# One count product and one copy for both neuron layers, and the middle turns written out

## What is computed

```python
def lif(x):                              # over time
    v = v + (xt - v) / TAU               # TAU = 2
    s = spike(v - VTH)                   # VTH = 1
    return (v * (1.0 - s), s)
x = x + lif(time_mix(layer_norm(x, ln1_s, ln1_b), ...))      # layer 0
x = x + lif(channel_mix(layer_norm(x, ln2_s, ln2_b), ...))   # layer 1
...
x = x + _layernorm(_L0_attn_ref(_layernorm(x), ...))
h = silu(lin(x, w1)) * lin(x, w2)
h = gelu(lin(h, h1)); h = gelu(lin(h, h2)); y = lin(h, w3)
x = x + _layernorm(_L0_ffn_ref(_layernorm(x), ...))
```

## Time and profile before

| what | value |
|---|---|
| runs, us | 679.1, 675.87, 678.21 (median 678.21) |
| profiled execution, span, us | 675.9 |
| instructions in the span | 10747 |
| granted TensorE clock, mean | 0.962 |
| busy, share of span: PE, DVE, ACT, POOL | 87%, 81%, 79%, 64% |
| DVE before the copy of `fired_all` (L1168), waiting for PE's sum | 40.2 us, 31 times |
| eight loop turns, us | 293.14 |
| the two turns after them, written out, us | 73.46 |

### The profile page before, as it was taken

The page is one execution under the profiler, slowest core; times in us unless marked ns, Lnnn a source line. Parts: engine busy times, 40 slices in busy tenths (PEclk is TensorE's granted clock), DMA queues, the critical chain, the costliest instruction groups (busy, mean ns, idle before and its releaser), DMA issues. The chain is left out here.

```text
span 675.9 us, 10747 instructions
## 1 busy us (share of the span) xinstructions
PE 587.6 (87%) x2241; PEld 365.2 (54%) x2241; DVE 549.4 (81%) x1532; ACT 536.8 (79%) x849; POOL 433.9 (64%) x576
## 2 busy tenths in 40 slices
PE   1246489999999999999999999999999999989783
PEld 0022146566655656575656665665657565656562
DVE  2865878989898998989898989899898989775631
ACT  4846377988989897979798898989797979857672
POOL 4323554687778685877768777868587774745352
PEclk9858889999999999999999999999999999999996
DMA  6110010001010100001010101010000101000000
GB/s 222 62 32 2 1 32 16 17 17 32 17 32 16 33 16 13 18 16 31 16 31 16 31 16 31 16 31 15 18 17 0 32 2 31 17 1 16 1 16 16
DMA packets 26538, 16.81 MB, mean 25 GB/s; under 512 B 1152, under 2 KB 25728, under 8 KB 26240
## 3 DMA queue, kind: packets, MB, share of 16 engines
q1 hardware_dynamic: 26496, 16.34, 7.9%
HBM read 12.14 MB, written 4.19 MB: 24 GB/s over the span
## 5 line engine op out<-in xcount | busy, mean ns | idle before, releaser
L780 ACT ACTIVATE hid<-p_f,scale 128x512 f32<-128x512 f32 x128 | 87.9, 687 | 64.9 <-PE p_f L1721 64.4
L1721 PE MATMUL p_f<-a_lo,w_hi 128*128 128x512 f32 x320 | 133.2, 416 | 3.0 <-DVE a_lo L293 1.7
L1721 PE MATMUL p_f<-a_hi,w_hi 128*128 128x512 f32 x320 | 125.9, 393 | 0.0
L1721 PE MATMUL p_f<-b_lo,w_hi 128*128 128x512 f32 x256 | 111.9, 437 | 3.6 <-DVE b_lo L293 2.3
L1721 PE MATMUL p_f<-b_hi,w_hi 128*128 128x512 f32 x256 | 100.5, 393 | 0.0
L427 POOL TENSOR_TENSOR rstd<-var,minus_half 128x4 f32<-128x4 f32 x64 | 84.9, 1326 | 2.5
L774 ACT ACTIVATE a_hi<-hid 128x512 fp32r<-128x512 f32 x128 | 79.1, 628 | 3.2 <-DVE hid L1260 1.5
L443 POOL TENSOR_TENSOR nd<-factors,pq 128x512 f32<-128x512 f32 x32 | 39.2, 1224 | 54.6 <-DVE pq L1127 54.5
L293 DVE TENSOR_TENSOR a_lo<-hid,a_hi 128x512 fp32r<-128x512 f32 x96 | 64.5, 696 | 10.5 <-ACT a_hi L774 10.4
L1721 PEld LDWEIGHTS p_f<-a_lo,w_hi 128*128 128x128 f32 x320 | 60.2, 188 | 23.1 <-issue 8.8
L293 POOL TENSOR_TENSOR b_lo<-hid,b_hi 128x512 fp32r<-128x512 f32 x32 | 46.5, 1467 | 39.1 <-ACT b_hi L774 34.7
(11 more groups left out here) (141 smaller groups left out, 1451.2 us busy)
## 6 DMA issues: line engine op xcount, KB each, us to landing
xa<-in_x SPq DMA_DIRECT2D x16, 256.0 KB, 2.8
xb<-in_x SPq DMA_DIRECT2D x16, 256.0 KB, 3.0
out<-y_out SPq DMA_DIRECT2D x16, 256.0 KB, 3.0
kk<-in_ffn SPq DMA_DIRECT2D x1, 1024.0 KB, 6.0
hid<-in_ffn SPq DMA_DIRECT2D x1, 1024.0 KB, 8.4
mix<-in_mix SPq DMA_DIRECT2D x1, 512.0 KB, 6.2
gate<-in_ffn SPq DMA_DIRECT2D x1, 512.0 KB, 4.0
mix<-in_mix SPq DMA_DIRECT2D x1, 320.0 KB, 3.8
```

Of the source, the lines that this page charges most:

```text
L780: act.activation(hid[:, m], p_f[m % 2][:, :], ACT.Gelu, scale=scale[:, 1 + layer, m:m + 1]).then_inc(s_gelu[layer], 1)
L1721: last = pe.matmul(out_, w[:, b], x[:, k], start=(k == 0 and t == 0), stop=(k == n - 1 and t == len(terms) - 1))
```

## The change

Two things are done.

First, `fired` and `fired_all` are one tile of two columns each, with one semaphore for the sum and one for the copy. `fired_sum` is one product of both columns for each turn, at the place where `fired_sum(1)` stood; it waits for both `fire`. `fired_flags` is one copy of two numbers behind `mix_1(0)`, where `fired_flag(0)` stood. Both `neurons` wait for that copy. POOL clears `fired` once at the start (one more memset, so the count of constants is 12).

Second, the loop is gone: turns 6 to 13 are written out with constants, on every engine. `g.edge` keeps PE's additional waits to the turns outside 6 to 13, where they were before.

```diff
-    def __init__(self, pair, step):
+    def __init__(self, pair, step, edge=True):
...
-        fired = [sb(f"fired{k}", [P, 1], BF16) for k in range(2)]
-        fired_all = [sb(f"fired_all{k}", [P, 1]) for k in range(2)]
+        fired = sb("fired", [P, 2], BF16)
+        fired_all = sb("fired_all", [P, 2])
...
             for i in range(first, last + 1):
-                if i == loop[0]:
-                    with fori(loop[0] // 2, len(loop) // 2 + loop[0] // 2) as pair:
-                        turn(groups(pair, 0), on(6))
-                        turn(groups(pair, 1), on(7))
-                elif i not in loop:
-                    which = first_turn if i < 3 else turn if i < GROUPS else last_turn
-                    which(groups(i // 2, i % 2), on(i))
+                which = first_turn if i < 3 else turn if i < GROUPS else last_turn
+                which(groups(i // 2, i % 2, not 6 <= i < GROUPS - 2), on(i))
...
             def neurons(k, g):
-                pool.wait_ge(s_fired_all[k], g.n + 1)
+                pool.wait_ge(s_fired_all, g.n + 1 + k)
                 pool.wait_ge(s_h_in[k], g.n + 1)
...
-            def fired_flag(k, g):
-
-                dve.wait_ge(s_fired_sum[k], g.n + 1)
-                wait(dve, s_spikes[k], g.n)
-                dve.tensor_copy(fired_all[k][0:1, :], p_m[0][0:1, 2 * k:2 * k + 1]).then_inc(s_fired_all[k], 1)
+            def fired_flags(g):
+
+                dve.wait_ge(s_fired_sum, g.n + 1)
+                wait(dve, s_spikes[0], g.n)
+                wait(dve, s_spikes[1], g.n - 1)
+                dve.tensor_copy(fired_all[0:1, :], p_m[0][0:1, 0:2]).then_inc(s_fired_all, 1)
...
                 if on[3]:
                     fire(1, g[3])
-                    fired_flag(1, g[3])
                 if on[2]:
                     fire(0, g[2])
                 if on[1]:
                     mix_1(g[1], 0)
-                if on[2]:
-                    fired_flag(0, g[2])
+                if on[2] or on[3]:
+                    fired_flags(g[2])
...
+                def fired_sum(g):
+
+                    after(pe, s_h_in[1], g.n - 1)
...
+                    after(pe, s_fired[0], g.n)
+                    after(pe, s_fired[1], g.n - 1)
+                    pe.matmul(p_m[0][:, 0:2], ones16[:, :], fired[:, :], start=True, stop=True).then_inc(s_fired_sum, 1)
...
-                    if on[3]:
-                        fired_sum(1, g[3])
+                    if on[2] or on[3]:
+                        fired_sum(g[2])
                     if on[4]:
                         hidden(1, g[4], 2)
-                    if on[2]:
-                        fired_sum(0, g[2])
                     if on[3]:
                         spikes_turned(1, g[3])
```

More of the change, by code:

```diff
@@ L50, in __init__ @@
         self.turn = pair + step // 2
+        self.edge = edge
 def after(eng, sem, n, per=1, nth=1):
[L55 to L59, removed]
+    if n < 0:
+        return
+    if n >= GROUPS_IN_ALL:
+        n, nth = GROUPS_IN_ALL - 1, per
     eng.wait_ge(sem, per * n + nth)
 def wait(eng, sem, count):
-    if not isinstance(count, int) or count > 0:
+    if count > 0:
         eng.wait_ge(sem, count)
@@ L248, in build @@
         s_spikes = [sem(f"s_spikes{k}") for k in range(2)]
-        s_fired_sum = [sem(f"s_fired_sum{k}") for k in range(2)]
-        s_fired_all = [sem(f"s_fired_all{k}") for k in range(2)]
+        s_fired_sum = sem("s_fired_sum")
+        s_fired_all = sem("s_fired_all")
         s_spk_tok = [sem(f"s_spk_tok{k}") for k in range(2)]
@@ L309, in build, with schedule, groups @@
         block = ctx.enter_context(nc.Block())
-        def schedule(fori, first_turn, turn, last_turn, first=-2, last=GROUPS + 3):
+        def schedule(first_turn, turn, last_turn, first=-2, last=GROUPS + 3):
             def on(i):
                 return {k: 0 <= i - k < GROUPS for k in range(-2, 5)}
-            def groups(pair, step):
-                return {k: Group(pair, step - k) for k in range(-2, 5)}
-            loop = range(6, GROUPS - 2)
+            def groups(pair, step, edge):
+                return {k: Group(pair, step - k, edge) for k in range(-2, 5)}
             for i in range(first, last + 1):
-                if i == loop[0]:
-                    with fori(loop[0] // 2, len(loop) // 2 + loop[0] // 2) as pair:
-                        turn(groups(pair, 0), on(6))
-                        turn(groups(pair, 1), on(7))
-                elif i not in loop:
-                    which = first_turn if i < 3 else turn if i < GROUPS else last_turn
-                    which(groups(i // 2, i % 2), on(i))
+                which = first_turn if i < 3 else turn if i < GROUPS else last_turn
+                which(groups(i // 2, i % 2, not 6 <= i < GROUPS - 2), on(i))
         @block.sync
@@ L361, in turn @@
             def turn(g, on):
-                if not isinstance(g[0].n, int) or 1 <= g[0].n < GROUPS - 2:
+                if 1 <= g[0].n < GROUPS - 2:
                     load_a(g[-2])
-                if on[0] and (not isinstance(g[0].n, int) or g[0].n > 0):
+                if on[0] and g[0].n > 0:
                     load_b(g[0])
@@ L634, in last_turn @@
                     shift_2(g[1])
-            schedule(pool.Fori, first_turn, turn, last_turn)
+            schedule(first_turn, turn, last_turn)
         @block.scalar
@@ L741, in relu @@
                 wait(act, s_fv, g.n)
-                if isinstance(g.n, int) and g.n == 0:
+                if g.n == 0:
                     act.wait_ge(s_rest[0], 1)
@@ L1004, in last_turn @@
                     inverse(g[1])
-            schedule(act.Fori, first_turn, turn, last_turn)
+            schedule(first_turn, turn, last_turn)
         @block.vector
@@ L2063, in last_turn @@
                         turn_5(g[4])
-                schedule(pe.Fori, first_turn, turn, last_turn, **turns)
+                schedule(first_turn, turn, last_turn, **turns)
             program(False, last=2)
```

145 lines of the change are left out of this document (62 added, 83 removed).

## The result

The changed kernel takes 693.97 us (median of four runs, 692.57 to 694.36) against 678.54 us for the kernel before on the same chip (675.87 to 679.1): the ratio is 1.0228, with an interval of 1.0204 to 1.0252. It is 15.4 us slower. The forecast was 681.2 us, with a range from 674.4 to 686.8, so the direction was right and the size far off.

What follows compares the result with a forecast made beforehand. The prediction took a ring of waits, not one full engine, to bound the kernel; -0.5 + 0.7 + 1.0 + 1.8 = +3.0 us on the median 678.21 gave 681.2 us, range 674.4 to 686.8.

Steps and rivals of the forecast that it cites:

- The waits as slack: DVE's waits before the copies (`fired_all`, 40.2 us, 2.62 per turn) are no gain: DVE would wait before `add_2` instead.
- the list of expected signs: Signs if right: 40.2 us shrink, waiting returns before `add_2`, middle turns 36.7 to 37.0 us, turn 3 longer by 1 to 1.5.
- PE's order sets this place: `add_2` and `add_1` on DVE wait for PE's turned tiles, dated by PE's place in its order, which the change leaves untouched.
- The second sum, -0.5: On PE, dropping the second sum saves 0.04 us in each of 12 full turns: -0.5 us.
- The loop, +0.7: Turns 6 to 13 written out take 36.73 us each instead of 36.64: +0.7 us, with ends -2.3 and +2.3.
- Rival 2: All turns take the short length, every `rstd(4)` at 1.39 us; faster, 674.9 us; chance 0.20.
- rival 4: The loop's jump back stalls engines, so writing it out gives back 2.3 us: 678.2 us; chance 0.04.
- The start-up, +1.0: In turn 3 the first transpose comes 1.5 us late, with nothing to fill in: +1.0 us, ends 0 and +1.5.
- Where the one copy falls, cost 0: The copy behind `mix_1(0)` ends at 512.80, allowing the transpose at 513.62, which PE reaches at 513.95: cost 0.
- 0.3 us of cover: Margin before PE's first transpose; if it goes, every further 0.1 us is 0.1 us of the turn.
- rival 1: POOL's `residual_5` takes the ports before `mix_1(0)`, transpose 0.67 us late: +9.2 in all, 687.4 us; chance 0.12.
- the freed POOL's 1.8 us: POOL's `low(2,0)` runs ahead of DVE's `low(2,1)`, making it 0.10 to 0.40 late: 0.15 × 12 = +1.8 us.

Runs made afterwards that it cites:

- The last experiment: Changed kernel with copy ahead of the mixing, transposes earlier, stats_3 ahead of low(2,1), residual_5 behind rstd(2): 684.94 us, ratio 1.0084 against the kernel before.

## Why the prediction was right or wrong

- **The waits as slack: right.** The 40.2 us before the copies were not to be had; DVE's waiting came back before `add_2`, with the transpose named, as the list of expected signs said. That PE's order sets this place holds: with the transposes earlier, `add_2` came 0.8 us sooner. The last experiment adds that the arm through hidden(1,3) and ACT's high part is only some 0.6 us shorter, and grows when the transposes move.
- **The second sum, -0.5: nothing.** The written-out turns with two sums and with one are equal (294.35 and 294.28 us for eight). The 0.04 us per turn reach `low(2,1)` and end there, because POOL still holds it by 0.2 us; an effect of this size could not be told from the noise of the totals either.
- **The loop, +0.7: about right,** measured +1.2 by the medians, with the turns near 36.75 but for one. Rival 2 (all turns short) and rival 4 (the jump was paid for) fall with it.
- **The start-up, +1.0: the delay right, the number in part luck.** The first transpose of turn 3 came 1.5 us later in the turn, as forecast. Turn 3 grew from 34.58 to 36.34 us, but it began 0.52 us sooner and turn 4 gave back 0.41, so that turn 5 begins 0.83 us later than before. Turn 3 of the kernel before, of the changed kernel, and of the run with the residual behind `low(2,2)`, which has the same late transpose:

```profile
68.84:103.42 34.58, 22.33 (x66) 10.63 (x64) 28.16 (x80) 20.54 (x32) 19.11 (x26) 0.85 0.05 16
68.32:104.66 36.34, 23.51 (x65) 11.04 (x63) 28.03 (x80) 20.57 (x32) 19.14 (x26) 0.77 0.05 15
69.08:103.34 34.26, 21.72 (x65) 10.21 (x63) 28.03 (x80) 20.45 (x32) 19.21 (x26) 0.85 0.06 16
```

  The third figure from the end is the granted TensorE clock, a mean over the turn. In the third run, at 0.85, the late transpose did not lengthen the turn, so what the start-up costs seems to go with the clock that the execution was granted; in the eight turns the clock is 1.00 in every window shown.
- **Where the one copy falls, cost 0: the step that failed.** The forecast let the mixing end in time for the copy and left 0.3 us of cover. "Lasts to about 512.65" took the mixing at its plain 0.75 us. It ran 1.78, the cover was gone, and the transposes waited. POOL won at a distance of 0.07 us, the very point from which rival 1 was said to decide, and I gave that rival 0.12. The evidence against it was one row, POOL at 135.12 and DVE at 135.24. That POOL operation reads one tile and numbers per partition, the residual reads two tiles; it was not the same kind of meeting. The row was no accident: in the changed kernel the same pair meets 13 times at 0.11 to 0.12 us, and DVE's operation takes its plain 0.69 us each time. The other row, at 549.09, was of the same two operations as the new meeting and went to POOL.
- **Rival 1's mechanism was right to the hundredth, its price too low: +9.2 for +15.4.** It forecast a transpose 0.67 us late, and 0.66 was measured. But I let the late transposes stand in place of the freed POOL's 1.8 us, which was itself too small. The runs showed that the two add up: the late copy brings `low(2,0)` to 0.50 us ahead of `low(2,1)`, and a DVE operation that comes sooner behind POOL's loses more. `low(2,1)` lost 0.66 us in most turns, where the forecast had 0.10 to 0.40 and took 0.15. With the copy ahead of the mixing it lost 0.2, as forecast. Taken away alone, this meeting is worth 7.3 us, and the first 11.5 us.

## What to carry to other kernels

A wait that is only slack may be what keeps two engines apart, or in the better order: `low(2,0)` and `low(2,1)` met in the kernel before as well, but DVE was 0.03 us ahead and POOL, which had slack, paid. Before such a wait is taken away, write down which operations will then start at nearly the same time on DVE and POOL, which is first, and how far apart. In the meetings of two-input operations here the loser pays most of the rest of the winner's time, so it pays most when it comes shortly behind; that price stands in the busy time of the instruction and in no list of waits. A small copy that others wait for belongs ahead of a large operation that may be held, not behind it.

## What the runs showed of the hardware

Where POOL's operation reads two tiles and starts first, the holding of DVE's two-input operation ends at a fixed time after POOL's start, whatever the distance from 0.07 to 0.96 us. With 0.75 and 0.68 us as the plain durations, the mixing came free 1.10 us after the start of the residual at a distance of 0.07 us (410.86 and 410.93) and 1.10 us after it at 0.31 (366.70 and 367.01). `low(2,1)` came free 1.16 us after `low(2,0)` started at a distance of 0.50 (414.14 and 414.64) and 1.18 at 0.96 (368.75 and 369.71). Behind the residual, in the experiment with the residual ahead of `low(2,0)`, `low(2,1)` came free at 1.16 too (369.50 and 369.82), so the small difference goes with DVE's operation. POOL's operations are recorded with 1.30 us each. The Trainium skill, page "SBUF — State Buffer", section "Who interferes with whom", has the lock for the whole instruction and the order of issue as what decides; the order agrees with every one of these rows, down to 0.07 us, and the release comes 0.1 to 0.2 us before POOL's recorded end. It agrees as well where DVE is first: at 514.98 and 515.01 `low(2,1)` ran its plain 0.68 us, and POOL's two low parts took 3.04 us together. The trace does not agree where POOL's operation reads one tile: at 135.12 and 135.24 POOL was first by 0.12 us, DVE's operation ran its plain 0.69 us, and POOL's took 0.96 us for a mean of 0.61.

It was also unexpected that the loop's alternation of 36.35 and 36.93 us is absent as soon as the turns are written out (36.75 nearly throughout). Why was not tried.
